# Spare identity products on TensorE in two waits of a four-layer gated block: between the recurrence's spread rows and behind the third combine's last product

## The chip, the cores and the metric

The kernel runs on one core of a Trainium2 chip, in one launch. The metric is device time in microseconds, lower is better. TensorE (PE) has a clock that the chip grants at one of two levels, 1.2 and 2.4 GHz; the profile shows it as PEclk 0.50 and 1.00. The other engines named here are VectorE (DVE), ScalarE (ACT), GpSimd (POOL) and SyncE (SP, which issues DMAs).

## The reference, cut to what matters

Eight sequences of 112 tokens, width 512, go through four layers; each layer is an attention-like part and an FFN, each behind a layernorm and a tanh gate. All data are fp32. The change touches the third layer and the border between the third and the fourth.

```python
# layer 2, attention part: a decayed recurrence over the context; only its mean is used
x = jnp.einsum('btd,ed->bte', kv, W_in) + b_in
_, states = lax.scan(lambda s, xt: (K * s + xt, K * s + xt), s0, jnp.swapaxes(x, 0, 1))
proj = jnp.einsum('btd,ed->bte', states, W_out) + b_out
y = Z + jnp.mean(proj, axis=1, keepdims=True)      # one row of 512 per sequence, spread over its tokens
return (y - mean(y)) / jnp.sqrt(var(y) + LN_EPS) * gamma + beta
...
# layer 2, FFN: mixture of 16 experts, 6 per token, and a shared expert (SwiGLU)
out = out + _swiglu(x, sw13, sw2)
...
x = x + jnp.tanh(g_xattn[3]) * _L3_xattn_ref(_layernorm(x), ...)   # layer 3 attention
```

## The kernel before

Tokens lie on partitions: `s.x[:, b, :]` is the 112 x 512 tile of sequence b (B = 8). The program is a row of stages, each a block in which every engine has its own hand-written list of instructions, and which ends when all engines have reached its end. Semaphores order the engines inside a stage. PSUM is eight banks of 512 fp32 columns, `s.bank[0]` to `s.bank[7]`.

**Recurrence stage** (`recurrence_stage`, layer 2's attention part). The eight context rows are ready in `s.state_rows` (8 x 512). For each sequence b TensorE multiplies a selector of 8 x 112 with them (line 2166, "spread row" b), so that bank b % 4 holds row b on all 112 token partitions. VectorE waits for it (`dve.wait_ge(spread, n + 1)`) and adds it to the normalized tile (line 2198); then come its statistics (2213, 2215), a reciprocal and a shift (2202, 2204). ACT normalizes the tile (2184), POOL multiplies by gamma (2158) and adds beta to x (2154), and VectorE adds the result to x (2210) and measures it for the next layernorm (272, 278). VectorE walks through the tiles in one software-pipelined loop `for n in range(B + 5)`, so its instructions stand in a fixed order. TensorE may run four spread rows ahead.

**After the recurrence** comes a layernorm stage (`measured_layernorm_stage`, here ln5): ACT and VectorE normalize, TensorE transposes 32 pieces with the identity (line 327), ACT copies them out (316); then the router's stage begins (line 469 and others).

**Combine stage** (`combine_stage`, one per mixture FFN; the third has top_k = 6). POOL gathers the experts' output rows, VectorE adds them to x (989), TensorE computes the shared expert. Its last products (line 956, in order 24, three for each tile) go to banks 4 to 7; VectorE adds them (1030) and measures. Behind the third combine stage the semaphores are cleared behind a barrier of all engines; then follow the layernorm stage ln6, whose transposes are again line 327, and layer 3's attention, whose first products (2289) wait for four weight matrices that SP starts to load in ln6 (2232).

Of the kernel before, what the change touches and what calls it, by code (L numbers as in the profile page):

```python
# [209 lines left out]
def layernorm_stage(nc, s, name):  # L210

    with ExitStack() as ctx:
        stats_done, mv_done, sd_done, rstd_done, norm_done, tr_done = s.sems(
            name, "stats_done", "mv_done", "sd_done", "rstd_done", "norm_done", "tr_done")
        copied = s.sems(name, "copied")[0]
        block = ctx.enter_context(nc.Block())

        @block.vector
        def _(dve):  # L220
            for n in range(B + 4):
                if n < B:
                    dve.bn_stats(s.stats[:, n, :], s.x[:, n, :]).then_inc(stats_done, 1)
                if 1 <= n < B + 1:
                    b = n - 1
                    dve.wait_ge(stats_done, b + 1)
                    dve.bn_aggr(s.mv[:, b, :], s.stats[:, b, :]).then_inc(mv_done, 1)
                if 3 <= n < B + 3:
                    b = n - 3
                    dve.wait_ge(sd_done, b + 1)  # L230
                    dve.reciprocal(s.rstd[:, b:b + 1], s.sd[:, b:b + 1]).then_inc(rstd_done, 1)
                if n >= 4:
                    b = n - 4
                    dve.wait_ge(rstd_done, b + 1)
                    dve.tensor_scalar(s.xn[:, b, :], s.x[:, b, :], s.mv[:, b, 0:1], s.rstd[:, b:b + 1],
                                      ALU.subtract, ALU.mult).then_inc(norm_done, 1)

        @block.scalar
        def _(act):
            for n in range(B + 3):  # L240
                if n < B:
                    act.wait_ge(mv_done, n + 1)
                    act.activation(s.sd[:, n:n + 1], s.mv[:, n, 1:2], ACT.Sqrt, bias=s.eps[0:TOK, :]).then_inc(sd_done, 1)
                if n >= 3:
                    b = n - 3
                    act.wait_ge(tr_done, b + 1)
                    act.activation(s.xnT[:, :, b * TOK:(b + 1) * TOK],
                                   s.bank[b % 4][:, 0:KD * TOK].rearrange("p (k t) -> p k t", k=KD), ACT.Copy)\
                       .then_inc(copied, 1)

        @block.tensor
        def _(pe):
            for n in range(B):
                pe.wait_ge(norm_done, n + 1)
                if n >= 4:
                    pe.wait_ge(copied, n - 3)
                for k in range(KD):
                    mm = pe.transpose(s.bank[n % 4][:, k * TOK:(k + 1) * TOK],
                                      s.xn[:, n, k * 128:(k + 1) * 128], s.ident[0:TOK, 0:TOK])
                mm.then_inc(tr_done, 1)  # L260

class Measure:
# [623 lines left out]
def combine_stage(nc, s, name, shared, layer, top_k, d=None):  # L887
# [7 lines left out]
    with ExitStack() as ctx:  # L895
# [17 lines left out]
        @block.sync  # L913
        def _(sp):
            if biases:
                sp.dma_start(bg[:, :], biases[0][:, E + 1, :]).then_inc(extra, 16)
                sp.dma_start(bu[:, :], biases[1][:, E + 1, :]).then_inc(extra, 16)

            if state:
                state.load(sp)  # L920
# [12 lines left out]
        @block.tensor  # L933
        def _(pe):
            pe.wait_ge(shared.loaded[1], 16 * 4)
            for q in range(PIECES):
                half, (f0, fn) = q // FC, chunks[q % FC]
                if q >= 2:
                    pe.wait_ge(h_done, q - 1)
                for weight, out, done in ((wg, s.bank[2 * (q % 2)], g_done), (wu, s.bank[2 * (q % 2) + 1], u_done)):  # L940
                    for k in range(KD):
                        mm = pe.matmul(out[0:fn, 0:HALF], weight[:, k, f0:f0 + fn],
                                       s.xnT[:, k, half * HALF:(half + 1) * HALF], start=(k == 0), stop=(k == KD - 1))
                    mm.then_inc(done, 1)
                if state and q == 1:
                    state.state_product(pe)
                if state and q == 3:
                    state.rows_product(pe)
            if state:
                pe.wait_ge(state.rows_copied, 1)  # L950
            for b in range(B):
                pe.wait_ge(h_done, FC * (1 + b // (B // 2)))
                if b >= 4:
                    pe.wait_ge(y_added, b - 3)
                for c, (f0, fn) in enumerate(chunks):
                    mm = pe.matmul(s.bank[4 + b % 4][0:TOK, :], hT[0:fn, c, b * TOK:(b + 1) * TOK], wd[0:fn, c, :],
                                   start=(c == 0), stop=(c == FC - 1))
                mm.then_inc(y_done, 1)

        @block.scalar  # L960
        def _(act):
# [320 lines left out]
def routed_ffn(nc, s, d, layer, top_k, width, func, softmax, eps, capacity=None, then_recurrence=False):  # L1282

    dram = tuple(d[f"l{layer}_{n}"] for n in ("wg", "wu", "wd"))
    biases = tuple(d[f"l{layer}_{n}"] for n in ("bg", "bu", "bd")) if layer == 0 else None
    bias_rows = d["l0_bias_rows"] if layer == 0 else None
    with ExitStack() as own:
        shared = Shared(nc, own, s, f"f{layer}", *dram, width, func, biases)
        with ExitStack() as of_ring:
            gate_loaded = s.sems(f"r{layer}", "gate_loaded")[0]  # L1290
            ring = Ring(nc, of_ring, s, f"f{layer}r", dram, width, bias_rows)

            def loads(sp):
                sp.dma_start(s.gate_w[:, :, 0:E], d[f"l{layer}_router"].rearrange("(k p) e -> p k e", p=128))\
                  .then_inc(gate_loaded, 16)
                load_shared(sp, shared, 0)

            measured_layernorm_stage(nc, s, f"ln{2 * layer + 1}", beside=loads, gate_loaded=gate_loaded)
            router_stage(nc, s, f"r{layer}", top_k, layer, softmax, eps, shared, ring, capacity)
            routed_blocks_stage(nc, s, f"f{layer}b", layer, top_k, ring, shared, width, func)  # L1300
        if then_recurrence:
            s.recurrence_vectors(own)
        combine_stage(nc, s, f"f{layer}c", shared, layer, top_k, d if then_recurrence else None)
        if then_recurrence:
            s.clear_semaphores()
            recurrence_stage(nc, s)
# [819 lines left out]
def recurrence_stage(nc, s):  # L2126
# [3 lines left out]
    with ExitStack() as ctx:  # L2130
# [14 lines left out]
        @block.gpsimd  # L2145
        def _(pool):
            pool.tensor_copy(select[:, :, :], s.ident[0:B, 0:B].unsqueeze(2).to_broadcast([B, B, TOK])).then_inc(selected, 1)
            for vector in (s.beta, s.gamma):
                pool.tensor_scalar(vector[:, :], vector[:, :], s.tanh_g[0:TOK, 2:3], None, ALU.mult).then_inc(scaled, 1)
            pool.wait_ge(scaled, 2)  # L2150
            for n in range(B + 3):
                if n < B:
                    pool.wait_ge(x_normed, n + 1)
                    pool.tensor_tensor(s.x[:, n, :], s.x[:, n, :], s.beta[:, :], ALU.add).then_inc(beta_added, 1)
                if n >= 3:
                    b = n - 3
                    pool.wait_ge(normed, b + 1)
                    pool.tensor_tensor(s.xn[:, b, :], s.xn[:, b, :], s.gamma[:, :], ALU.mult).then_inc(weighted, 1)

        @block.tensor  # L2160
        def _(pe):
            pe.wait_ge(selected, 1)
            for b in range(B):
                if b >= 4:
                    pe.wait_ge(row_added, b - 3)
                pe.matmul(s.bank[b % 4][0:TOK, :], select[:, b, :], s.state_rows[:, :], start=True, stop=True)\
                  .then_inc(spread, 1)

        @block.scalar
        def _(act):  # L2170
# [640 lines left out]
```

## Time and profile before

| | us |
|---|---|
| median of 3 runs | 2526.84 (2520.09 to 2531.94) |
| the profiled execution's own time | 2530.18 |
| its span | 2528.4 |
| mean granted TensorE clock | 0.964 of full |
| PE busy | 2335.0 (92%) |
| DVE busy | 1021.3 (40%) |

The times above are of whole executions. The span is that of the profiled execution, from its first to its last instruction. Busy time of PE says that products were in flight, not that it ran at its peak.

### The profile page before, as it was taken

How to read it: one execution, taken by the hardware profiler on the slowest of the kernel's cores; microseconds unless marked ns; L12 is line 12 of the kernel's file. 1: busy time of each engine (PE TensorE's matmuls, PEld its weight loads, DVE VectorE, ACT ScalarE, POOL GpSimd, SP SyncE). 2: the span in 40 equal slices, each digit the busy share in tenths (PEclk: the TensorE clock that was granted, in tenths of full speed). 3: DMA queues.
4: the chain of work that ended last, by engine and by line, in shares of the span. 5: the costliest groups of instructions: out<-in, count | busy, mean ns of one | idle time of the engine just before them, and what ended most of it. 6: DMA issues, size and time to landing. Idle time of an engine off the chain costs nothing. (4 is left out here: it accounts for less than half of the span.)

```text
span 2528.4 us, 33898 instructions
## 1 busy us (share of the span) xinstructions
PE 2335.0 (92%) x9778; PEld 1382.9 (55%) x9779; DVE 1021.3 (40%) x2555; ACT 715.9 (28%) x1671; POOL 382.9 (15%) x528
## 2 busy tenths in 40 slices
PE   7899999988888899998999999599999999699898
PEld 4444444444655566666455554255655555346586
DVE  5645455444334333345522224771222223602375
ACT  2445353530110566665011110301111110151221
POOL 6000000001122100000011115301111112500151
PEclk9999999998999999999999999699999999899899
DMA  9401010022773000002256645143444442551220
GB/s 328 130 1 34 0 34 0 0 83 93 244 245 122 29 18 10 10 14 91 90 188 199 195 142 158 42 140 107 146 157 135 152 155 90 162 185 37 87 88 29
DMA packets 170882, 263.63 MB, mean 104 GB/s; under 512 B 13326, under 2 KB 106894, under 8 KB 170285
## 3 DMA queue, kind: packets, MB, share of 16 engines
q1 hardware_dynamic: 139821, 185.96, 23.0%
q0 software_dynamic: 16000, 49.30, 6.6%
q10 hardware_dynamic: 14976, 27.27, 2.9%
q8 instruction: 50, 0.82, 0.1%
q14 instruction: 35, 0.29, 0.0%
HBM read 212.68 MB, written 49.81 MB: 104 GB/s over the span
## 5 line engine op out<-in xcount | busy, mean ns | idle before, releaser
L1157 PE MATMUL bank<-f2r_wd,f2b_hT 128*128 (+1 forms) x300 | 137.2, 593 | 1.4 <-DVE f2b_hT L1261 1.4
L1138 PE MATMUL bank<-f2r_wg,f2b_xT 128*128 x400 | 129.2, 467 | 2.0 <-issue 2.0
L1138 PE MATMUL bank<-f2r_wu,f2b_xT 128*128 x400 | 127.1, 461 | 0.0
L1595 PE MATMUL bank<-l0a_vo,l0a_zT 128*112 128x512 f32 x256 | 115.5, 594 | 2.9 <-DVE l0a_zT L1756 2.9
L1248 DVE TENSOR_TENSOR f2b_h<-bank,f2b_acted 128x352 f32<-128x352 f32 x50 | 26.2, 525 | 203.3 <-PE bank L1138 203.3
L1659 ACT ACTIVATE l0a_p<-l0a_p,l0a_low 112x375 f32<-112x375 f32 x128 | 77.2, 607 | 91.0 <-DVE l0a_low L1749 89.9
L1138 PEld LDWEIGHTS bank<-f2r_wu,f2b_xT 128*128 128x128 f32 x400 | 76.5, 191 | 42.9 <-issue 1.0
L1739 DVE CUSTOM_DVE_ANT_0 l0a_p<-bank,xn 112x375 f32<-112x375 f32 x128 | 70.3, 549 | 70.6 <-PE bank L1567 39.9
L1565 PE MATMUL bank<-l_kvcT,xnT 128*112 128x375 f32 x256 | 92.3, 482 | 5.0 <-ACT xnT L1688 5.0
L2488 POOL TENSOR_SCALAR f_below<-l_raw,l_half 128x512 f32<-128x512 f32 x33 | 58.4, 1783 | 233.5 <-POOLq L286 197.0
L1926 PEld LDWEIGHTS bank<-l1w_v,ctxT 128*125 128x125 f32 x768 | 88.7, 188 | 8.5 <-issue 0.6
L1138 PEld LDWEIGHTS bank<-f2r_wg,f2b_xT 128*128 128x128 f32 x400 | 73.1, 193 | 35.1 <-issue 4.0
L1157 PE MATMUL bank<-f1r_wd,f1b_hT 128*128 (+1 forms) x192 | 87.9, 593 | 1.4 <-DVE f1b_hT L1261 1.4
L1926 PE MATMUL bank<-l1w_v,ctxT 128*125 128x128 f32 x768 | 89.1, 273 | 0.0
L1201 ACT ACTIVATE f2b_acted<-bank 128x352 f32<-128x352 f32 x50 | 23.2, 464 | 230.2 <-PE bank L1138 230.2
L327 PE MATMUL bank<-ident,xn 112*128 112x112 f32 x192 | 33.9, 365 | 57.8 <-DVE xn L304 57.8
L1915 PE MATMUL bank<-ctxT,l1w_k 128*128 128x375 f32 x256 | 86.1, 478 | 0.2 <-ACT l1a_pT L2040 0.2
L1138 PE MATMUL bank<-f1r_wg,f1b_xT 128*128 x256 | 83.2, 469 | 1.5 <-ACT f1b_xT L1194 1.2
L1253 DVE COPY f2b_y<-bank 128x512 f32<-128x512 f32 x50 | 34.6, 692 | 123.3 <-PE bank L1157 123.3
L2503 PE MATMUL bank<-f_xr,f_tern 128*128 128x448 f32 x352 | 74.6, 372 | 6.9 <-DVE f_tern L2558 5.4
L1138 PE MATMUL bank<-f1r_wu,f1b_xT 128*128 x256 | 81.0, 459 | 0.0
L1157 PEld LDWEIGHTS bank<-f2r_wd,f2b_hT 128*128 128x128 f32 (+1 forms) x300 | 53.3, 191 | 49.7 <-issue 49.4
(408 smaller groups left out, 4439.8 us busy)
## 6 DMA issues: line engine op xcount, KB each, us to landing
slot_rows<-zeros SPq DMA_DIRECT2D x2, 7424.0 KB, 41.8
slot_rows<-f2b_y ACTq DMA_DIRECT2D x50, 256.0 KB, 3.8
f1r_wg<-in_l_wg SPq DMA_DIRECT2D x16, 704.0 KB, 4.4
f1r_wu<-in_l_wu SPq DMA_DIRECT2D x16, 704.0 KB, 5.9
f2r_wg<-in_l_wg SPq DMA_DIRECT2D x16, 704.0 KB, 4.5
f2r_wu<-in_l_wu SPq DMA_DIRECT2D x16, 704.0 KB, 5.9
xn<-in_l_w_ffn SPq DMA_DIRECT2D x11, 768.0 KB, 4.4
l_raw<-in_l_w_ffn SPq DMA_DIRECT2D x11, 768.0 KB, 4.4
```

Of the source, the lines that this page charges most:

```text
L327: mm = pe.transpose(s.bank[b % 4][:, k * TOK:(k + 1) * TOK], s.xn[:, b, k * 128:(k + 1) * 128], s.ident[0:TOK, 0:TOK])
L1138: mm = pe.matmul(bank[:, 0:width], xT[:, v, k, :], w[:, bass.ds(at, 1), k, :].rearrange("p o f -> p (o f)"), start=(k == 0), stop=(k == KD ...
L1157: mm = pe.matmul(bank_y[v][:, :], hT[0:fn, v, c, :], wd[0:fn, bass.ds(at, 1), c, :].rearrange("p o f -> p (o f)"), start=(c == 0), stop=(c ...
L1253: dve.tensor_copy(y[:, v, :], bank_y[v][:, :]).then_inc(y_copied, 1)
L1565: pe.matmul(s.bank[j][0:TOK, 0:T], qT[:, j, toks], a.kvcT[:, keys], start=True, stop=False)
L1595: mm = pe.matmul(s.bank[7][0:TOK, :], zT[:, b % 2, j, :], vo[:, j, :], start=(j == 0), stop=(j == GH - 1))
L1659: act.activation(p[:, b % 2, j, :], p[:, b % 2, j, :], ACT.Exp, bias=low[:, b % 2, j:j + 1], scale=SCALE0, accum_out=total[:, b % 2, j:j + ...
L1739: dve.tensor_tensor_reduce(out=p[:, b % 2, j, :], in0=s.bank[j][0:TOK, 0:T], in1=a.mask[:, b, :], scale=1.0, scalar=-3.0e38, op0=ALU.add, ...
L1915: mm = pe.matmul(bank_k[:, 0:T], w.k[:, k, :], s.ctxT[:, k, b * T:(b + 1) * T], start=(k == 0), stop=(k == KD - 1))
L1926: mm = pe.matmul(bank_v[0:TT, t * VB:(t + 1) * VB], s.ctxT[:, k, b * T + t * TT:b * T + (t + 1) * TT], w.v[:, k, :], start=(k == 0), stop= ...
L2488: pool.tensor_scalar(below[:, i % 2, :], t.raw[:, c % RAWS, m, :], t.half[:, 3 + m:4 + m], None, ALU.is_lt).then_inc(below_done, 1)
L2503: mm = pe.matmul(s.bank[2 * (n % 2) + m][:, 0:HALF], tern[:, c % TERNS, m, k * 128:(k + 1) * 128], xr[:, part, k, halves(half)], start=(pa ...
```

## The change

A helper issues plain products of the 128 x 128 identity with the identity repeated four times (512 columns). They write a PSUM bank that nobody reads at that point, signal no semaphore and wait for none. Two of them stand behind each of the eight spread rows, six more behind the last, and ten behind the third combine stage's last product: 32 calls in all.

```diff
+def keep_busy(pe, s, bank, times):
+
+    for _ in range(times):
+        pe.matmul(s.bank[bank][:, :], s.ident[:, :], s.ident[:, :].unsqueeze(1).to_broadcast([128, 4, 128]),
+                  start=True, stop=True)
@@ combine_stage, tensor @@
                     mm = pe.matmul(s.bank[4 + b % 4][0:TOK, :], hT[0:fn, c, b * TOK:(b + 1) * TOK], wd[0:fn, c, :],
                                    start=(c == 0), stop=(c == FC - 1))
                 mm.then_inc(y_done, 1)
+            if top_k == 6:
+                keep_busy(pe, s, 0, 10)
@@ recurrence_stage, tensor @@
                 pe.matmul(s.bank[b % 4][0:TOK, :], select[:, b, :], s.state_rows[:, :], start=True, stop=True)\
                   .then_inc(spread, 1)
+                keep_busy(pe, s, 7, 2)
+            keep_busy(pe, s, 7, 6)
```

TensorE's list in the recurrence stage, from the second combine's last products on. Before, with the eight spread rows in one row of the list:

```order
L956 MATMUL bank<-f_shared_d,f1c_hT 112x512 x24
L895 UNCONDITIONAL_BRANCH
L2160 UNCONDITIONAL_BRANCH
L2166 MATMUL bank<-state_rows,l2r_select 112x512 x8
L2130 UNCONDITIONAL_BRANCH
L320 UNCONDITIONAL_BRANCH
L327 MATMUL bank<-ident,xn 128x112 x28
```

The same place now (the spread rows are line 2175 there, the spare products line 266; the rows left out repeat the pair):

```order
L963 MATMUL bank<-f_shared_d,f1c_hT 112x512 x24
L902 UNCONDITIONAL_BRANCH
L2169 UNCONDITIONAL_BRANCH
L2175 MATMUL bank<-state_rows,l2r_select 112x512
L266 MATMUL bank<-ident 128x512 x2
...
L2175 MATMUL bank<-state_rows,l2r_select 112x512
L266 MATMUL bank<-ident 128x512 x8
L2139 UNCONDITIONAL_BRANCH
L327 UNCONDITIONAL_BRANCH
```

Each spread row but the first now stands behind two more calls than its predecessor, 14 for the last; eight calls stand between the last one and the transposes.

TensorE's list at the end of the third combine stage, now:

```order
L963 MATMUL bank<-f_shared_d,f2c_hT 112x512 x24
L266 MATMUL bank<-ident 128x512 x10
L902 UNCONDITIONAL_BRANCH
L327 UNCONDITIONAL_BRANCH
L334 MATMUL bank<-ident,xn 128x112 x32
```

The second of these rows is new; nothing else in the list moved, and no other engine's list changed.

## Rows read from the trace of the kernel before

**Rows 1.** The page: span, and PE's busy time.

```profile
span 2528.4 us, 33898 instructions
...
PE 2335.0 (92%) x9778; PEld 1382.9 (55%) x9779; DVE 1021.3 (40%) x2555; ACT 715.9 (28%) x1671; POOL 382.9 (15%) x528
```

**Rows 2.** Busy time by stretch around the recurrence (us, then x instructions).

```profile
core 0: us, PE busy (x) PEld busy (x) DVE busy (x) ACT busy (x) POOL busy (x), PEclk, DMA share, GB/s
...
1615.00:1620.00 5.00, 0.00 (x0) 0.00 (x0) 4.83 (x13) 1.41 (x3) 3.52 (x3) 0.50 0.01 2
...
1645.00:1650.00 5.00, 5.00 (x11) 2.42 (x11) 4.51 (x35) 1.97 (x3) 0.00 (x0) 0.76 1.01 311
```

**Rows 3.** Timeline of PE, 1593 to 1640: start, us, instruction, idle before it.

```profile
1592.52 1.45 PE L956 MATMUL bank<-f_shared_d,f1c_hT 128*112 128x512 f32 x3
1598.93 13.99 PE L2166 MATMUL bank<-state_rows,l2r_select 8*112 8x512 f32 x16 [4.96 <-POOL l2r_select L2147]
1633.35 4.74 PE L327 MATMUL bank<-ident,xn 112*128 112x112 f32 x28 [20.42 <-DVE xn L304]
```

**Rows 4.** Timeline of DVE, 1599 to 1633: additions of rows 0, 5, 7, and the end.

```profile
1601.19 0.69 DVE L2198 TENSOR_TENSOR xn<-xn,bank 112x512 f32<-112x512 f32 x1 [0.88 <-ACT xn L2175]
...
1611.44 0.67 DVE L2198 TENSOR_TENSOR xn<-xn,bank 112x512 f32<-112x512 f32 x1
...
1613.09 1.83 DVE L2210 TENSOR_TENSOR x<-x,xn 112x512 f32<-112x512 f32 x1
...
1619.53 0.67 DVE L2198 TENSOR_TENSOR xn<-xn,bank 112x512 f32<-112x512 f32 x1
...
1631.70 0.18 DVE L278 BATCH_NORM_AGGREGATE mv<-stats 112x2 f32<-112x6 f32 x1
```

**Rows 5.** Passes of 512 columns, by source line: ns min/median/max, first and last start.

```profile
L2166 PE MATMUL bank<-state_rows,l2r_select x16: 1056/1056/1188, 1598.9 to 1611.9; 8*112 8x512 f32 x16
...
L956 PE MATMUL bank<-f_shared_d,f1c_hT x48: 590/592/596, 1573.2 to 1593.4; 128*112 128x512 f32 x32, 96*112 96x512 f32 x16
```

**Rows 6.** Busy time by stretch where the clock fell and rose around the recurrence.

```profile
1592.00:1596.20 4.20, 1.98 (x5) 0.53 (x3) 3.93 (x8) 0.00 (x0) 0.00 (x0) 1.00 0.00 0
1596.20:1637.10 40.90, 17.74 (x36) 8.47 (x37) 34.52 (x77) 18.28 (x31) 24.27 (x19) 0.50 0.08 24
```

**Rows 7.** Busy time by stretch before and after other rises of the clock.

```profile
592.70:596.00 3.30, 3.30 (x5) 1.07 (x4) 3.19 (x6) 0.00 (x0) 0.31 (x2) 0.50 0.00 0
596.20:600.00 3.80, 3.80 (x9) 1.16 (x8) 1.41 (x2) 0.00 (x0) 2.19 (x2) 1.00 0.34 81
685.30:688.20 2.90, 2.90 (x7) 2.36 (x8) 0.00 (x0) 0.00 (x0) 0.00 (x0) 0.50 1.07 386
```

**Rows 8.** Timeline of PE, 582 to 600 (L520 has 18 rows, L522 is dense).

```profile
590.76 2.04 PE L520 MATMUL bank<-r_bd,r_gT 18*112 18x512 f32 x2
592.73 3.63 PE L522 MATMUL bank<-f_shared_d,r_hT 128*112 128x512 f32 x4
```

**Rows 9.** Busy time by stretch around the third combine stage's end.

```profile
2170.00:2175.00 5.00, 3.70 (x9) 1.03 (x7) 2.27 (x4) 0.00 (x0) 3.82 (x4) 1.00 0.67 180
...
2188.60:2193.50 4.90, 0.20 (x1) 0.00 (x0) 4.79 (x10) 0.00 (x0) 3.68 (x5) 1.00 0.55 167
2193.60:2205.60 12.00, 0.00 (x0) 0.00 (x0) 9.01 (x21) 1.58 (x2) 1.82 (x2) 0.50 0.29 84
2205.60:2210.50 4.90, 4.89 (x26) 4.89 (x27) 3.15 (x7) 2.83 (x6) 0.00 (x0) 0.50 0.93 340
...
2217.20:2220.80 3.60, 3.60 (x5) 1.80 (x6) 0.00 (x0) 0.00 (x0) 0.00 (x0) 0.50 0.76 310
```

**Rows 10.** Timeline of PE, 2170 to 2222.

```profile
2205.61 5.70 PE L327 MATMUL bank<-ident,xn 112*128 112x112 f32 x32 [16.81 <-DVE xn L304]
2217.15 5.09 PE L2289 MATMUL bank<-xnT,l3w_q 128*128 128x448 f32 x8 [5.85 <-DMA l3w_o<-in_l_w_oT]
```

**Rows 11.** Timeline of DVE, 2186 to 2222: its last work in the third combine stage.

```profile
2201.58 0.30 DVE L278 BATCH_NORM_AGGREGATE mv<-stats 112x2 f32<-112x6 f32 x3
```

## The prediction

> **What bounds the kernel now.** I read the page first: a span of 2528.4 us with PE busy for 92% of it [rows 1]. An average says nothing of two short places, so I went on to the stretches there. In the recurrence PE has nothing more to do from about 1613 on, while DVE is busy for 4.83 of 5 us [rows 2, 3]: DVE's fixed list of instructions sets the length of this stage. It runs from 1601.19, where row 0 is added, to 1631.9 [rows 4], and the next stage's transposes begin at 1633.35, after PE has waited 20.4 us [rows 3]. Behind the third combine PE is done at 2188.8 and waits 16.8 us for DVE, whose last work there ends near 2201.9 [rows 9 to 11]. So neither wait is PE's own; PE matters there only if it comes late, or if its clock is worth something afterwards.
>
> The clock: PE's last dense product before the recurrence ends at 1593.97, the clock falls at 1596.2, and it stays at 0.50 (1.2 GHz) for 40.9 us [rows 3, 6]. In that time PE ran the 16 passes of the spread rows without a break for 14 us [rows 3]. They use 8 of 128 array rows, and did not bring the clock up. I take from this that the spread rows don't help, whatever stands between them.
>
> **What a spare call costs.** It is a plain fp32 product with 512 columns, so two passes. At full clock 47 intervals between the second combine's passes of that width take 1593.4 - 1573.2 = 20.2 us, 0.43 us each; at the low clock the 15 intervals between the spread passes take 13.0 us, 0.86 each [rows 5]. A call costs 0.86 us at 2.4 GHz and 1.72 us at 1.2 GHz.
>
> **Part 1, two calls behind each spread row.** The spares need nothing from the others, but PE works in order and DVE's additions stand behind the spread rows. At the low clock a round (a row and two spares) takes 6 x 0.86 = 5.16 us. Row 0 is ready at 1598.93 + 1.72 + 0.2 = 1600.85 (0.2 is the 1.06 us that a pass lasts less its interval), row n at 1600.85 + 5.16 n: row 5 at 1626.65, row 7 at 1636.97. DVE now adds row 5 at 1611.44 and row 7 at 1619.53 [rows 4]. At full clock a round takes 2.58 us. From row 0's addition to row 5's DVE itself takes 10.25 / 5 = 2.05 us for a round, so even at full clock the spread rows would pace the first five additions. From row 5's to row 7's DVE takes 8.1 us, more than two rounds at full clock (5.2) and less than two at the low one (10.3): row 5 decides when the clock is up, row 7 when it is not.
>
> So all hangs on whether, and when, the spares lift the clock. If it rises at time r, what was left of the low-clock schedule takes half: row 5 is ready at (1626.65 + r) / 2. Rises elsewhere in this trace came after runs of dense or full products of 2.9 us (from 685.3), 3.4 us (from 592.73), 3.8 us (from 1633.35) and 4.9 us (from 2205.6) [rows 3, 6 to 9]. The one from 592.73 is instructive: ahead of it stood products of 18 rows, and the clock was at 0.50 when they ended; it rose only after four unbroken dense passes [rows 7, 8]. The spares give exactly such runs: four passes, 3.44 us, broken by 1.72 us of an 8-row product. That is at the edge of the four cases, two of which would fit in one run. Where the first run (from 1600.65) does it, r = 1604.1, row 5 comes at 1615.4, and the stage is 3.9 us longer. Where the second does it (from 1605.81), r = 1609.2, row 5 comes at 1617.9, 6.5 us late. Once up it should hold: between 2170 and 2175 PE was busy for 3.70 of 5 us, near the two thirds that dense passes take here, with the clock at 1.00 [rows 9]. DVE may win a little back. Its addition at 1613.09 took 1.83 us, one of the same size 0.67 [rows 4], with POOL at work beside it; if POOL is ahead by then, up to 1.2 us goes. I take 0.7. The two cases give +3.2 and +5.8, and I take **+4.5 us**.
>
> **Part 2, six calls at the end.** With the clock up, row 7's round begins near 1620 and eight calls of 0.86 us end near 1627. The transposes would start at 1633.35 + 4.5 = 1637.9: some 10 us of nothing. The clock fell after 2.2 us of idle PE at 1596.2 and after 4.7 us at 2193.5 [rows 3, 6, 9]. So it is low again when the transposes come, as before. These calls lie under 10 us of DVE's work and cost nothing: **0**. Were that cover gone they would cost 5.2 us.
>
> **Part 3, ten calls behind the third combine.** The clock is at 1.00 there; they last 8.6 us, from 2188.8 to 2197.4, under DVE's work, which ends at 2201.9 and holds the barrier [rows 9, 11]. Cover left over: 4.5 us. The transposes start at 2205.6, 8.2 us after the last spare, beyond both waits after which the clock fell. Even a warm clock would end nowhere: layer 3's first products wait for a weight matrix until 2217.15 [rows 10]. **0**.
>
> Sum against the profiled execution's own time: 2530.18 + 4.5 = 2534.7. That execution lies 3.3 us above the median of the runs, so for the median I say 2526.84 + 4.5 = **2531 us**. Half a per cent, 12.6 us, is about what a measurement of this kernel tells from no change.
>
> **Rival 1: the clock stays low through the spread rows.** For it: the runs of 3.44 us are cut by products that did not lift the clock in 14 us, and two of four rises above needed longer. Against it: eight runs in a row, and a 2.9 us run that was enough. Price: row 7 ready at 1636.97 against 1619.53, +17.4, less 0.7: **+16.7 us**, 2543.5. The last eight calls would then be unbroken, lift the clock and end near 1645, still under DVE, whose end goes to 1648.6. It decides from where a rise needs more than about 3.4 us of unbroken dense passes: 27%.
>
> **Rival 2: faster, because the clock carries over.** The low spells ahead of which spares now stand hold 3.8 us (from 1633.35), 0.24 / 0.5 x 5 = 2.4 us (router, 1645 to 1650), 4.9 us (from 2205.6) and 3.6 us (from 2217.2) [rows 2, 3, 6, 9]. At full clock each would halve, if nothing else bounded it: 7.4 us at most. For it: the spares shorten PE's idle times from 20.4 and 16.8 us to some 10 and 8. Against it: the clock fell after 2.2 and 4.7 us. It needs a clock that holds through 8 to 10 us of idle, and less than 3 us lost on the rows; then 2526.84 - 7.4 + 3 = 2522, inside half a per cent. 7%.
>
> **Rival 3: nothing.** DVE takes up the wait with its own slack: rows come when it would have been held by POOL anyway, within 1.5 us of before, 2528. 6%.
>
> **How the numbers follow.** Forecast 60%, rivals 27, 7 and 6%. Slower by over half a per cent is rival 1 and nearly nothing of the forecast: 0.26. Faster by so much needs rival 2 and luck: 0.03. The rest, 0.71. The likeliest case alone spans 2527 to 2536 (+1.5 to +7 and a median that wanders by some 2 us). The range takes in rivals 1 and 3: 2524 to 2546.
>
> **What would show it.** In the profile of the changed kernel: the recurrence's 44 spare passes at intervals of 0.86 us at first and 0.43 after a rise between 1603 and 1611; the recurrence's additions waiting for PE at rows 1 to 5, where before only ACT was waited for; the stage's end, and ln5's transposes, 3 to 7 us later; PEclk at 0.50 when both sets of transposes start; the tail behind the third combine unchanged. The prediction is wrong if the clock is still at 0.50 at row 7 (then the stage is 17 us longer), or if it is at 1.00 when ln5 or ln6 begins.

## The result, and the profile after

Over 20 runs each, the changed kernel takes 2534.61 us (median, 2530.45 to 2540.6) and the kernel before 2528.72 us (2520.09 to 2534.17). The ratio is 1.0023, 95% interval 1.0015 to 1.0032: 5.9 us slower, real but inside the half per cent. The forecast was +4.5 us and 2531, with a range of 2524 to 2546. Of the 3.6 us between 2531 and 2534.61, 1.9 come from the median before, which was 2526.84 over three runs. The profiled execution of the changed kernel took 2530.56 us, one of the shortest, so its total hides the loss: its first spread row starts 1.2 us earlier than in the trace of before, and from the router's first product to ln6's transposes it takes 557.7 us against 562.0. There the trace of before is the odd one; those of all other kernels lie between 556.3 and 559.6. I therefore read both traces from an event that the change doesn't touch, the start of the first spread row.

The timeline of PE in the changed kernel; line 2175 is the spread row, 266 the spare calls, 334 ln5's transposes:

```profile
1597.70 2.04 PE L2175 MATMUL bank<-state_rows,l2r_select 8*112 8x512 f32 x2 [5.17 <-POOL l2r_select L2156]
1599.68 3.78 PE L266 MATMUL bank<-ident 128*128 128x512 f32 x4
1603.39 1.11 PE L2175 MATMUL bank<-state_rows,l2r_select 8*112 8x512 f32 x2
1604.43 1.98 PE L266 MATMUL bank<-ident 128*128 128x512 f32 x4
1606.35 1.11 PE L2175 MATMUL bank<-state_rows,l2r_select 8*112 8x512 f32 x2
1607.38 1.98 PE L266 MATMUL bank<-ident 128*128 128x512 f32 x4
...
1622.14 7.13 PE L266 MATMUL bank<-ident 128*128 128x512 f32 x16
1637.71 4.47 PE L334 MATMUL bank<-ident,xn 112*128 112x112 f32 x28 [8.44 <-DVE xn L311]
```

From the first row to the first transpose it is 1637.71 - 1597.70 = 40.0 us; before it was 1633.35 - 1598.93 = 34.4 [rows 3]. **The stage is 5.6 us longer**, nearly the whole 5.9. A round at full clock takes 1606.35 - 1603.39 = 2.96 us, not 2.58: four spare passes take 1.92 instead of 1.72, and the two passes of a row 1.04 instead of 0.86.

The clock, by stretches of the changed kernel (us, PE, PEld, DVE, ACT, POOL busy, PEclk):

```profile
1596.80:1603.40 6.60, 5.70 (x7) 1.63 (x7) 2.26 (x5) 4.71 (x7) 6.51 (x6) 0.50 0.00 0
1603.60:1634.10 30.50, 25.68 (x54) 8.68 (x53) 25.17 (x57) 10.97 (x19) 17.66 (x14) 1.00 0.00 1
1634.30:1641.00 6.70, 3.29 (x18) 3.29 (x19) 5.80 (x14) 1.94 (x5) 0.00 (x0) 0.50 0.43 121
1641.10:1645.00 3.90, 3.69 (x36) 2.44 (x38) 0.62 (x1) 2.31 (x5) 0.00 (x0) 1.00 0.97 345
```

It rose with the end of the first run of spares, near 1603.5, where it had stayed low for 40.9 us before [rows 6]. It fell again near 1634.2, 4.9 us after the last spare and 3.5 us ahead of the transposes. The mean granted clock of the profiled execution went from 0.964 to 0.973, and bought nothing.

DVE's wait for PE in the changed kernel's stage, from its table of waits (us in total, times, longest):

```profile
DVE xn L2209 <- PE bank L2175: 6.5, 5, 3.0
```

The timeline of DVE there: the additions of rows 5 and 7; between them the addition of the first finished tile to x and a shift.

```profile
1616.41 0.69 DVE L2209 TENSOR_TENSOR xn<-xn,bank 112x512 f32<-112x512 f32 x1 [0.23 <-PE bank L2175]
...
1617.50 0.68 DVE L2221 TENSOR_TENSOR x<-x,xn 112x512 f32<-112x512 f32 x1
...
1620.49 1.28 DVE L2215 SCALAR_TENSOR_TENSOR l2r_shift<-mv,rstd 112x1 f32<-112x1 f32 x1
...
1623.90 0.67 DVE L2209 TENSOR_TENSOR xn<-xn,bank 112x512 f32<-112x512 f32 x1
```

Before, none of DVE's waits in this stage was for PE. Now the additions of rows 1 to 5 wait 6.5 us for it. Row 5 is added 18.7 us after the first row's start, against 12.5 [rows 3, 4]: 6.2 us late. From row 5's addition to row 7's DVE now takes 7.49 us, where it took 8.09: 0.6 us is won back, and 5.6 is left. It is a balance of three instructions: the addition to x takes 0.68 us instead of 1.83 and the shift ahead of it 0.37 instead of 0.94, but the shift at 1620.49 takes 1.28 us, and the same one took 0.16 before.

The timeline of PE behind the third combine, changed kernel:

```profile
2185.57 8.75 PE L266 MATMUL bank<-ident 128*128 128x512 f32 x20
2205.32 6.03 PE L334 MATMUL bank<-ident,xn 112*128 112x112 f32 x32 [11.00 <-DVE xn L311]
2217.33 13.09 PE L2300 MATMUL bank<-xnT,l3w_q 128*128 128x448 f32 x29 [5.98 <-DMA l3w_o<-in_l_w_oT]
```

Busy time and clock by stretch, right behind the last call and then from the fall of the clock on:

```profile
2194.30:2197.30 3.00, 0.02 (x1) 0.00 (x0) 3.00 (x7) 0.00 (x0) 1.20 (x1) 1.00 0.48 116
2197.50:2211.00 13.50, 5.67 (x31) 5.68 (x32) 8.03 (x18) 5.00 (x9) 0.00 (x0) 0.50 0.53 178
```

The ten calls last 8.75 us, PE then idles 11 us, the clock falls 3 us after the last call, and the transposes run low as before [rows 9, 10]. Layer 3's first products wait for the same weight matrix.

### The profile page after: what moved, and what is told of

It is laid out like the page before. It is cut to its first block and busy times, and to the rows that moved or that the text cites. A ratio compares the mean times of both kernels' runs of the same rounds, so it can differ in the third digit from the quotient of the medians.

```text
span 2528.8 us, 34026 instructions
## 1 busy us (share of the span) xinstructions
PE 2356.6 (93%) x9842; PEld 1390.5 (55%) x9843; DVE 1020.9 (40%) x2555; ACT 715.3 (28%) x1671; POOL 383.2 (15%) x528
```

## The experiments

Each kernel starts from the changed one; all but third_only and carry_both also leave out the ten calls behind the third combine. For each I give the ratio to the kernel before, measured on the same chip (medians of before 2529.85 to 2530.7); a difference in us behind it is worked out from the ratio. From its trace, a single execution, I give the **stage**: first spread row to first transpose, 34.4 us before. It repeats: third_only, tail_only, dense_rows, carry_rec and dense_carry, which have no spares between the rows, all gave 34.4 us again.

**Which part costs: the recurrence's 22 calls alone.**

```diff
-            if top_k == 6:
-                keep_busy(pe, s, 0, 10)
```

> The recurrence's 22 calls alone, without the ten behind the third combine. Theory 1 (the whole loss is the spread rows coming late to VectorE): about +5.9 us against before, as the full change; in the profile the recurrence's first spread row to the end of VectorE's work there takes about 38.5 us, against 33.0 before. Theory 2 (the ten calls behind the third combine cost a part, by holding the barrier or by disturbing the gathers): clearly less than +5.9, say +3.

Measured: 2539.37 against 2530.70, ratio 1.0037 (1.0023 to 1.0051). The stage takes 1643.49 - 1603.39 = 40.1 us, +5.7:

```profile
1603.39 2.05 PE L2173 MATMUL bank<-state_rows,l2r_select 8*112 8x512 f32 x2 [5.03 <-POOL l2r_select L2154]
1605.37 3.78 PE L266 MATMUL bank<-ident 128*128 128x512 f32 x4
1609.08 1.19 PE L2173 MATMUL bank<-state_rows,l2r_select 8*112 8x512 f32 x2
...
1643.49 4.50 PE L334 MATMUL bank<-ident,xn 112*128 112x112 f32 x28 [8.45 <-DVE xn L311]
```

That is its timeline of PE. The schedule is that of the full change, and the interval of the ratio (+5.8 to +12.9 us) reaches down to it. The medians differ by 8.7 us, more than the stage explains; of the 9.2 us between the two profiled executions 4.5 lie ahead of the first spread row (1603.39 against 1598.93), where both kernels do the same. So the recurrence's calls carry the loss.

**The ten calls behind the third combine alone.**

```diff
-                keep_busy(pe, s, 7, 2)
-            keep_busy(pe, s, 7, 6)
```

> The ten calls behind the third combine alone. Theory 1: 0 within 1 us; the last call ends about 8.6 us after the last shared product, some 4 us before VectorE's last work in the stage; the clock is at 0.50 again when ln6's transposes begin. Theory 2: +1 us or more. A third view (they keep the clock up for ln6): -1 to -2 us, and PEclk 1.00 at the transposes.

Measured: 1.0004 (0.9994 to 1.0013). They ran for 8.75 us from 2187.49 and left PE idle for 10.9 us; the clock was low from 2198.6 to 2212.3, with the transposes starting at 2207.15. Nothing lost or won.

**Only the six calls behind the last row.**

```diff
-            if top_k == 6:
-                keep_busy(pe, s, 0, 10)
...
-                keep_busy(pe, s, 7, 2)
```

> Only the six calls behind the last spread row; nothing between the rows. Theory 1: 0 within 1 us, since rows come as before and the calls lie under VectorE's work; they last about 5 x 1.72 us at the low clock and end near 1622, 10 us ahead of the transposes, which start at 0.50. Rival (late end of TensorE's list, or traffic in PSUM, slows VectorE): +1 us or more.

Measured: 1.0005 (0.9996 to 1.0014); the stage takes 1637.55 - 1603.18 = 34.4 us, as before. The twelve passes were faster than I expected, 7.2 us, since the clock rose about 3.5 us into them. So of the recurrence's calls those between the rows cost, and those behind cost nothing.

**Spares of 8 rows instead of 128.** The same number of calls, each a product of the selector with the context rows.

```diff
-                keep_busy(pe, s, 7, 2)
+                for _ in range(2):
+                    pe.matmul(s.bank[7][0:TOK, :], select[:, 0, :], s.state_rows[:, :], start=True, stop=True)
-            keep_busy(pe, s, 7, 6)
+            for _ in range(6):
+                pe.matmul(s.bank[7][0:TOK, :], select[:, 0, :], s.state_rows[:, :], start=True, stop=True)
```

> As rec_only, but each spare call is a product of the 8-row selector with the context rows, of the same 512 columns, instead of 128 rows of identity. If 8-row products don't lift the clock: PEclk 0.50 from before the first row to ln5's transposes, rounds of 6 x 0.86 = 5.16 us, the last row 17 us late, +17 us against before (the price put on rival 1). If any unbroken stream of products lifts it: rounds of 2.6 us after the first, and +4 us. It also tells where the round of 2.95 us in the changed kernel comes from: if from the change between 8-row and 128-row products, rounds here are an exact multiple of a pass (5.16 us low, or 2.58 high); if from the semaphore wait or signal at each row, 0.2 to 0.4 us more.

Measured: 1.0070 (1.0056 to 1.0083), +17.7 us (15.0 by the medians); the stage takes 53.0 us, +18.6. Row 7 is added 17.4 us late, and 1.2 us more is the tail, which now ends last. Its busy time and clock by stretch:

```profile
1598.20:1656.00 57.80, 55.42 (x81) 22.09 (x82) 30.88 (x75) 18.18 (x31) 23.89 (x19) 0.50 0.06 18
1656.30:1660.00 3.70, 3.49 (x35) 2.01 (x33) 0.62 (x1) 1.83 (x4) 0.00 (x0) 1.00 0.82 284
```

Its timeline of PE, one round and the start of the next (2176 is the spare product):

```profile
1604.39 1.91 PE L2173 MATMUL bank<-state_rows,l2r_select 8*112 8x512 f32 x2
1606.10 3.62 PE L2176 MATMUL bank<-state_rows,l2r_select 8*112 8x512 f32 x4
1609.51 1.91 PE L2173 MATMUL bank<-state_rows,l2r_select 8*112 8x512 f32 x2
```

PE was busy for 55.4 of 57.8 us, 51.5 of them with 8-row products from 1599.13 on, and the clock stayed at its lower level all the time. Rounds are 5.12 us, six passes of 0.853 with nothing between them. That is the schedule that the price of rival 1 was worked out from, and it says where the 0.38 us that a round of the changed kernel takes too long are not: not in a row's semaphores.

**Rows of 128 instead of 8, with the spares.**

```diff
-            for n, rows in (("state_rows", B), ("gamma", TOK), ("beta", TOK)))
+            for n, rows in (("state_rows", 128), ("gamma", TOK), ("beta", TOK)))
...
+        dve.memset(s.state_rows[:, :], 0.0).then_inc(self.zeroed, 1)
...
-        select = sb("select", [B, B, TOK])
+        select = sb("select", [128, B, TOK])
...
-s.ident[0:B, 0:B].unsqueeze(2).to_broadcast([B, B, TOK])
+s.ident[:, 0:B].unsqueeze(2).to_broadcast([128, B, TOK])
```

> As rec_only, but the selector and the context rows are padded with zeros to 128 rows, so that the spread rows are 128-row products like the spares. If the 0.37 us over six passes in each round comes from changing between 8-row and 128-row products, rounds are 2.58 us at full clock, row 5 is about 1.9 us earlier than in rec_only, and the time against before is about +4 us instead of +5.9. If it comes from the semaphore signal or wait of a spread row, rounds stay at 2.95 and the time too. The clock should rise at least as early, since PE then has one unbroken run of dense products.

Measured: 1.0011 (1.0002 to 1.0020), +2.8 us; the stage takes 38.0 us, +3.6. Its timeline of PE, one round:

```profile
1609.09 1.02 PE L2176 MATMUL bank<-state_rows,l2r_select 128*112 128x512 f32 x2
1609.95 1.88 PE L266 MATMUL bank<-ident 128*128 128x512 f32 x4
1611.67 1.02 PE L2176 MATMUL bank<-state_rows,l2r_select 128*112 128x512 f32 x2
```

A round is now 2.58 us, as I had reckoned. So each change between an 8-row and a 128-row product costs about 0.19 us, two in a round. The number of columns of the left operand, 112 and 128, changes here as well, and costs nothing that shows.

**One spare call between rows.**

```diff
-                keep_busy(pe, s, 7, 2)
+                keep_busy(pe, s, 7, 1)
```

> One spare call between rows instead of two, six behind the last, none at the third combine. If the clock rises only after about 3 us or more of unbroken 128-row products, runs of 1.72 us don't lift it: PEclk stays 0.50 until the tail, rounds take 3.44 + 0.4 to 0.5 us, row 5 comes about 8.5 us late, and the time is +8 us against before: half the spare work costs more than all of it. If the cost goes with the work that is put in, it is +3 us or less and the clock is up by the third row.

Measured: 1.0040 (1.0026 to 1.0054); the stage takes 43.8 us, +9.4. Busy time and clock by stretch:

```profile
1600.00:1634.40 34.40, 34.32 (x36) 8.97 (x37) 19.24 (x51) 14.05 (x25) 20.54 (x17) 0.50 0.00 0
1634.60:1638.40 3.80, 3.80 (x9) 1.33 (x7) 3.66 (x8) 0.81 (x1) 2.36 (x2) 1.00 0.00 0
```

PE was busy without a gap, and up to the last row half of its passes had 128 rows, yet the clock rose only in the tail, near 1634.5. Half of the spare calls between the rows make the stage 3.7 us longer than all of them do. The times of the whole kernel don't tell the two apart: this interval overlaps that of rec_only. A round is 3.98 us here (from the row at 1604.05 to the next at 1608.03), four passes of 0.86 and two changes, so a change costs about 0.27 us at the low clock.

**Four spare calls between rows.**

```diff
-                keep_busy(pe, s, 7, 2)
+                keep_busy(pe, s, 7, 4)
```

> Four spare calls between rows instead of two, six behind the last, none at the third combine. The clock rises within the first run (6.9 us long at the low clock); rounds at full clock are ten passes and two changes, 4.3 + 0.37 = 4.67 us. Row 1 comes near 1607, row 7 near 1635 on before's time scale, 15.5 us late: +15 us against before. If VectorE, not PE, had set the pace of the changed kernel, it would be nearer to +6.

Measured: 1.0059 (1.0045 to 1.0072), +14.9 us; the stage takes 1651.10 - 1600.63 = 50.5 us, +16.1. The clock rose within the first run, rounds take 4.67 us, and every addition from row 1 on waits 1.5 to 4.7 us for PE. So PE, not DVE, sets the pace of the additions.

**Rows of 128 and no spares at all.** With the padding of above:

```diff
-                keep_busy(pe, s, 7, 2)
-            keep_busy(pe, s, 7, 6)
```

> The kernel before with only its selector and context rows padded with zeros to 128 rows; no spare calls at all. If it is the rows used that decide whether products lift the clock, the 16 passes of the spread rows now lift it: PEclk goes to 1.00 within 3 to 7 us of the first, where in the kernel before 14 us of the same passes with 8 rows left it at 0.50. VectorE sets the pace anyway, so the time is 0 within 2 us. If the clock stays at 0.50, something else about the spread rows (their waits, their source) is the cause.

Measured: 1.0002 (0.9993 to 1.0010); the stage takes 34.4 us. Busy time and clock by stretch, from the first row on:

```profile
1602.50:1607.50 5.00, 5.00 (x6) 1.98 (x7) 3.06 (x7) 3.78 (x7) 4.92 (x4) 0.50 0.00 0
1607.70:1612.10 4.40, 4.40 (x11) 1.54 (x9) 4.26 (x11) 2.27 (x5) 4.40 (x5) 1.00 0.00 0
```

The clock rose 5.1 us into the same sixteen passes, with zeros in 120 more rows.

**What a warm clock is worth: calls up to the end of both waits.**

```diff
-                keep_busy(pe, s, 0, 10)
+                keep_busy(pe, s, 0, 19)
...
-                keep_busy(pe, s, 7, 2)
-            keep_busy(pe, s, 7, 6)
+            keep_busy(pe, s, 7, 19)
```

> Nothing between the rows; 19 calls behind the last row and 19 behind the third combine, so many that PE works until about VectorE's last instruction in each stage. It asks what a clock that is up at the transposes would be worth (rival 2). PE idles only 2 to 4 us ahead of each set of transposes. If the clock holds, transposes run in about 3 us instead of 4.7 to 5.7 and the first of them are at 1.00: -1 to -3 us against before, at most the 7.4 us of rival 2. If it falls all the same, or ACT's copies set the pace of the transposes, 0; if the calls end late in some executions, +1 us.

Measured: 0.9996 (0.9987 to 1.0006). Its timeline of PE; 476 is the router stage's first product:

```profile
1616.76 19.50 PE L266 MATMUL bank<-ident 128*128 128x512 f32 x38
1637.70 3.34 PE L334 MATMUL bank<-ident,xn 112*128 112x112 f32 x28 [1.45 <-DVE xn L311]
...
1646.53 4.94 PE L476 MATMUL bank<-xnT,f_shared_g 128*128 128x448 f32 x8 [0.30 <-PEq L293]
```

With 1.45 us of idle the clock held. From the first transpose to the router's first product it is 8.8 us, against 1643.57 - 1633.35 = 10.2 before (10.0 to 11.4 in the other traces): 1.4 us won. ACT's first seven copies ran back to back there, in 3.28 us, beside 3.34 us of transposes, so a faster PE would have won little more. The stage itself is 34.9 us: the calls ended 0.4 us too late. Net 1.0 us, less than the times can tell. The high clock went no further: it fell again at 1646.6, and the router's first eight products take 4.94 us, as in the kernel before. Ahead of them stand small products. Behind the third combine PE idled 3.8 us, the clock was still at 1.00 then and fell as ln6's transposes began; they took 4.95 us instead of 5.70, and layer 3's first products still waited 6.8 us for their weight matrix.

**The same in the recurrence alone, with 18 calls.**

```diff
-                keep_busy(pe, s, 7, 2)
-            keep_busy(pe, s, 7, 6)
+            keep_busy(pe, s, 7, 18)
```

> As carry_both with 18 calls behind the last row, and none behind the third combine. If the third combine's calls are worth nothing (layer 3's first products wait for their weights), the same as carry_both: -1 us, within 2. If they are worth what the warmer transposes of ln6 show, carry_both is 1 us or more faster than this one.

Measured: 1.0001 (0.9991 to 1.0010). The last call ended 3.1 us ahead of the transposes, and the clock fell as they began; the calls in the timeline of PE, and busy time by stretch:

```profile
1610.76 17.37 PE L266 MATMUL bank<-ident 128*128 128x512 f32 x36
```

```profile
1628.20:1631.10 2.90, 0.00 (x0) 0.00 (x0) 2.18 (x7) 0.30 (x1) 0.00 (x0) 1.00 0.00 0
1631.30:1634.60 3.30, 3.30 (x18) 3.30 (x19) 3.07 (x7) 1.72 (x4) 0.00 (x0) 0.50 0.91 251
```

The calls last 17.37 us, two passes less than in carry_both but 2.1 us less time. TensorE's list is the same up to there, but the clock rose 3.4 us into the calls here and 5.9 us into them in carry_both (3.5 in tail_only): **the time of the rise differs between executions**. The two kernels' intervals overlap, so the third combine's calls show no worth either.

**Rows of 128, 24 calls behind the last.** With the padding of above:

```diff
-                keep_busy(pe, s, 7, 2)
-            keep_busy(pe, s, 7, 6)
+            keep_busy(pe, s, 7, 24)
```

> Rows padded to 128, nothing between them, 24 spare calls behind the last, none at the third combine: rows come on time, the clock is up from early on, and PE works until 1 to 3 us before VectorE's end. If an idle of about 2 to 3 us leaves the clock up, ln5's transposes run at 1.00 and the stretch from the first transpose to the router's first product takes 8.8 us instead of 10.2: -1 to -1.5 us against before, too little to be told from nothing by the times; the stretches in the profile decide. If the clock falls ahead of them: 0.

Measured: 0.9987 (0.9978 to 0.9997), -3.3 us, the only ratio here below one by its interval. I had expected nothing if the clock fell ahead of the transposes, and it did. The last call ended 4.2 us ahead of the transposes, which began at 0.50; the stage took 34.4 us, and first row to router 45.2 us, against 44.6 before: nothing was won there. Its trace is shorter than that of before between the router's first product and ln6's transposes (556.3 us against 562.0), but so are those of all other kernels, as said above. I can't call the ratio a gain of the calls: with eleven comparisons one interval may miss by chance, and no second measurement of it was made.

## Why the prediction was right, point by point

**The mechanism** was as forecast: PE works in order, the rows stand behind the spares, DVE waits for rows 1 to 5, row 5 decides, and the stage's end moves by that. rec_only, tail_only and third_only put the loss on the calls between rows; one and four calls show that both the clock and the calls' work set the pace.

**When the clock rises.** I gave two cases, a rise in the first or in the second run of spares. In both traces with two 128-row calls between 8-row rows (the full change and rec_only) it was the first, 3.8 us into it, as the run ended. With one call between the rows the clock stayed low for all eight rows, 30 us; with two it rose in both traces. Whether the length of a run or the share of 128-row passes makes the difference, no run tells. Nor is the second case ruled out for other executions, since the time of the rise differed by 2.5 us between traces of one list (tail_only, carry_both, carry_rec). The first case alone would have given +3.2.

**The mis-sized term: "at full clock a round takes 2.58 us".** It takes 2.96. The change between an 8-row and a 128-row product costs 0.19 us, and 0.26 at the low clock (1599.68 - 1597.70 less two passes of 0.86; 0.27 in one_between). My sum had nothing for it. Ten of them stand ahead of row 5: about 2 us. That is most of the difference between the first case's +3.9 for row 5 and the measured +6.2; with padded rows row 5 came 4.1 us late. My +4.5 came near 5.9 only because I averaged in a second case that occurred in neither trace: the forecast's size was luck in part. The sign was in the trace of before: the two 18-row passes ahead of 592.73 took 1.97 us there [rows 8], 0.26 more than two passes at the low clock, and I used the rows for the clock alone.

**What DVE wins back**: 0.7 us taken, 6.2 - 5.6 = 0.6 measured. The addition gave back 1.15, as I had thought it might; that a later shift took 1.1 us longer I had not seen, so the net is luck.

**Parts 2 and 3 at nothing**: shown by tail_only and third_only; their intervals leave room for +3.5 us at most, and the stage of tail_only is as long as before. The clock fell 4.9 and 3 us after the last spares, ahead of both sets of transposes.

**Rival 1** did not occur in the traces. eight_rows stands in for it: row 7 came 17.4 us late, as in my sum, the 0.7 us that I had taken off didn't come back, and the whole cost +17.7 (15.0 by the medians). With 128-row spares at the low clock it would have cost more, since 14 changes stand ahead of row 7: 14 x 0.27 = 3.8 us by my estimate. **Rival 2** did not either. Its bound of 7.4 us was far too high: where the clock did hold into ln5 it was worth 1.4 us, as ACT's copies pace the transposes and the clock fell again ahead of the router. **Rival 3** is ruled out by the 6.5 us of waiting.

**The rule on transposes.** The Trainium skill, page "TensorE: Matmul & The Clock Gate", Part 4, says that transposes don't count as busy PE in the way that products do. The traces don't agree: the changed kernel's clock rose at 1641 in the middle of ln5's transposes too. And it rose at 1603.5 behind products of identity with identity. They are not what a transpose sends through the array, as I had written: that is the data and the identity (`bank<-ident,xn`). Had the spares counted for nothing, the time would have been rival 1's.

## What to carry to other kernels

Spare products cost nothing here behind the last product that somebody waits for. Between products that others wait for, each pushes the next one back by its whole length as soon as TensorE is the slower of the two, and it is twice as long while the clock is low. Count the work between two needed products against the consumer's own round (up to 2.45 us for these rows) before asking about the clock. And a high clock has a value only if it reaches the next dense stretch: here it was still up after 1.45 us of idle and fell after 3.1, and the stretch was paced by another engine anyway. These are single traces; elsewhere in them the clock fell after idle times from 2.2 to 4.9 us.

## What the runs showed that I had not expected

- Products of 8 rows did nothing for the clock: 51.5 us of unbroken passes left it at its lower level. With the spread rows padded with zeros to 128 rows it rose 5.1 us after the first of them, at no cost that the times show (1.0002, 0.9993 to 1.0010).
- A change between 8-row and 128-row products costs 0.19 us at the high clock and 0.26 to 0.27 at the low one; between 96-row and 128-row products none shows, at 0.43 us a pass [rows 5].
- Half the spare work between the rows cost more than all of it in the stage: +9.4 us with one call, +5.7 with two, +16.1 with four.
- The clock's rise is no fixed time behind the same list of products: 3.4, 3.5 and 5.9 us into the same calls in three traces.
